# Edge softmax of the third graph layer: lanes of 128 edges, turned by TensorE, in place of a table in memory

## The reference

```
h = (x @ W.T).reshape(n, 8, 64)
e = leaky_relu(e_src + e_dst, 0.2)          # one number per edge and head
e = e * (1.0 + et_emb[edge_type]) * edge_weight[:, None]
e_max = zeros(n, 8).at[dst].max(e)          # maximum over the edges of a node, at least 0
e = exp(e - e_max[dst])
e_sum = zeros(n, 8).at[dst].add(e)
out = zeros.at[dst].add(h[src] * e / (e_sum[dst] + 1e-10)) + x
```

## Time and profile before

| | us |
|---|---|
| median of 3 runs | 1818.19 (1817.63 to 1823.83) |
| profiled execution | 1826.41 |
| its span, first to last instruction | 1824.3 |
| TensorE busy | 1594.4 (87%) |
| VectorE busy | 898.4 (49%) |
| GpSimd busy | 642.5 (35%) |

### The profile page before, as it was taken

The page is one execution under the profiler, slowest core; times in us unless marked ns, Lnnn a source line. Parts: engine busy times, 40 slices in busy tenths (PEclk is TensorE's granted clock), DMA queues, the critical chain, the costliest instruction groups (busy, mean ns, idle before and its releaser), DMA issues.

```text
span 1824.3 us, 23037 instructions
## 1 busy us (share of the span) xinstructions
PE 1594.4 (87%) x7110; PEld 880.6 (48%) x7111; DVE 898.4 (49%) x2199; ACT 501.0 (27%) x1607; POOL 642.5 (35%) x748
## 2 busy tenths in 40 slices
PE   6989999998697999999993496679699899999698
PEld 3534444446354546464551373524244455555455
DVE  8878888887634443433433035978722101011322
ACT  1134444446422414232230112411210211111233
POOL 5867787772332322223233812537500000000000
PEclk9999999998798999999996697579899999999899
DMA  7030101006323142222212572566515222210020
GB/s 308 4 103 24 58 24 58 24 7 169 84 71 125 53 90 78 79 84 56 86 37 87 131 250 79 163 149 186 162 69 190 69 75 69 98 58 23 10 60 18
DMA packets 132572, 162.75 MB, mean 89 GB/s; under 512 B 62041, under 2 KB 74601, under 8 KB 132114
## 3 DMA queue, kind: packets, MB, share of 16 engines
q1 hardware_dynamic: 105888, 116.45, 20.6%
q0 software_dynamic: 18752, 29.91, 6.2%
q10 hardware_dynamic: 7858, 15.44, 2.5%
HBM read 145.87 MB, written 15.88 MB: 89 GB/s over the span
## 4 chain that ended last, share of the span: by engine, by line
PE 69%; DMA 14%; DVE 11%; issue 3%; ACT 2%; POOL 1%; DVEq 0%; ACTq 0%; POOLq 0%
PE psum L377 68%; DMA tab_sorted<-rec,pos 12%; DVE arena L2586 2%; DVE stats L468 1%; DVE ring L1277 1%; PE psum L1008 1%; PE psum L2245 0%; POOL arena L624 0%; DMA arena<-tab_x 0%; DMA tab_x<-xn,gate 0%; POOL tab_x L2288 0%; ACT arena L2837 0%; DMA x<-in_x 0%; DVE xn L2038 0%; DVE mv L469 0%
## 5 line engine op out<-in xcount | busy, mean ns | idle before, releaser
L377 PE MATMUL psum<-arena 128*128 128x24 bf16 (+8 forms) x2026 | 325.8, 319 | 30.8 <-DVE arena L654 12.8
L377 PE MATMUL psum<-arena,ring 128*128 (+1 forms) x1504 | 325.4, 363 | 9.3 <-issue 6.2
L377 PE MATMUL psum<-xT,ring 128*128 128x384 f32 x928 | 319.4, 506 | 10.1 <-ACT ring L3020 4.2
L377 PEld LDWEIGHTS psum<-arena 128*128 128x128 bf16 (+5 forms) x2026 | 199.3, 149 | 163.5 <-issue 74.7
L377 PE MATMUL psum<-ring,arena 128*128 128x512 f32 (+1 forms) x592 | 271.1, 605 | 7.3 <-ACT arena L2837 3.8
L377 PE MATMUL psum<-ring,xT 128*128 128x512 f32 x552 | 252.3, 609 | 2.9 <-DMA bc<-in_wide 1.8
L377 PEld LDWEIGHTS psum<-xT,ring 128*128 128x128 f32 x928 | 182.4, 198 | 140.6 <-issue 30.0
L377 PEld LDWEIGHTS psum<-arena,ring 128*128 128x128 bf16 (+1 forms) x1504 | 139.2, 115 | 130.3 <-issue 28.9
L2128 POOL DMA_INDIRECT tab_sorted<-rec,pos x104 | 99.9, 961 | 242.6 <-DMA tab_sorted<-rec,pos 226.0
L1059 ACT ACTIVATE ring<-ring 128x128 f32<-128x128 f32 x416 | 123.3, 297 | 173.3 <-DVE ring L1343 173.3
L377 PEld LDWEIGHTS psum<-ring,arena 128*128 128x128 f32 (+1 forms) x592 | 102.6, 187 | 133.7 <-issue 132.6
(11 more groups left out here) (456 smaller groups left out, 1635.4 us busy)
## 6 DMA issues: line engine op xcount, KB each, us to landing
ring<-in_L_ffn_w SPq DMA_DIRECT2D x22, 1024.0 KB, 8.3
ring<-in_L_gnn_m_w SPq DMA_DIRECT2D x8, 1024.0 KB, 6.1
ring<-in_L_ffn_expert_weights SPq DMA_DIRECT2D x8, 1024.0 KB, 5.4
ring<-tab_key ACTq DMA_DIRECT2D x24, 256.0 KB, 3.2
ring<-in_L_gnn_Wv SPq DMA_DIRECT2D x5, 1024.0 KB, 5.1
tab_w<-xn SPq DMA_DIRECT2D x6, 768.0 KB, 14.4
ring<-in_L_gnn_Ww SPq DMA_DIRECT2D x4, 1024.0 KB, 17.1
ring<-in_L_gnn_wq SPq DMA_DIRECT2D x4, 1024.0 KB, 6.3
```

The source lines that it names most:

```text
L377: return nc.tensor.matmul(o, a, b, start=start, stop=stop)
```

## The change

- `rec` is no longer loaded for this layer; scores, factors and keys use `rec2`, so column T is tile T (25 groups still, the last of two tiles). `edge_factors` waits for the tile-wise load.
- The destination key is the number within its chunk. One compare instead of three serves it; TensorE picks the chunk's table with a register, loaded by `chunks_of` once a group, after the wait for the compares. A group has four compares and 16 matmuls of 24 columns.
- Leaky ReLU and factor: GpSimd does tiles 0 to 39 ahead of its gather 13, and tiles 40 to 79 ahead of gather 21 (four operations each); VectorE does the last 18 tiles, waiting for GpSimd (`factored`) ahead of its multiply.
- TensorE transposes the scores, eight times 128 x 98 to 98 x 128, into two banks; VectorE's scans read them there: 16 scans over 98 partitions x 128. The scan over lanes is 8 x 196.
- The joining is 16 operations of 98 x 128, in two halves of four heads; after each half come the subtraction, four transposes on TensorE and the exponential on ScalarE, which writes `w_tile`. `tab_weight`, its store and its two loads are gone.
- The clearing matmuls of the scatter and the first `hot` (7 tiles) with its bf16 form come earlier, beside the scans and the `l2m` step.

```diff
-        GG = EW // GT
+        GG = (TT2 + GT - 1) // GT
+        HH = H8 // 2
+        POOLED_SCORES = {13: (0, 10), 21: (10, 20)}
+        SCORED_LATE = GT * 20
@@ sp
-            sp.wait_ge(ex_done, 1)
-            sp.dma_start(tab_weight.rearrange("(p t) h -> p t h", p=P), weight[:]).then_inc(weights_stored, 16)
-            sp.wait_ge(weights_stored, 16)
...
-                sp.dma_start(w_tile[:, T0:T1, :], tiles_of_weights[:, T0:T1, :]).then_inc(weights_in[part], 16)
@@ pe, a group of scores
                 pe.wait_ge(nodes_ready, g + 1)
                 b = banks.open(pe, f"l2e{g}")
-                for j in range(GT):
-                    for f in range(2):
-                        for c in range(NT):
...
+                four = chunks_of(GT * g)
+                for j in range(min(GT, TT2 - GT * g)):
+                    o = b[:, j * 3 * H8:(j + 1) * 3 * H8]
+                    for c in range(NT):
+                        mm(o, node_hot[:, g % 2, c, j * P:(j + 1) * P], parts[:, 0, c, :, :].rearrange("p k h -> p (k h)"),
+                           c == 0, False)
+                    last = mm(o, node_hot[:, g % 2, NT, j * P:(j + 1) * P], dst_parts[:, bass.ds(four[j] * 3 * H8, 3 * H8)], False, True)
@@ pe, after the scores
             pe.wait_ge(lanes_ready, 1)
+            banks.at = SUMS + 1
+            for k in range(2):
+                b = banks.open(pe, f"l2t{k}")
+                for h in range(HH):
+                    last = nc.tensor.transpose(b[0:TT2, h * P:(h + 1) * P], w_edge[:, :, HH * k + h], ident[:])
+                last.then_inc(banks.full_of(f"l2t{k}"), 1)
+            pe_clear_sums(pe, "l2")
...
+            for k in range(2):
+                pe.wait_ge(lanes_ready, 4 + k)
+                b = banks.open(pe, f"l2v{k}")
+                for h in range(HH):
+                    last = nc.tensor.transpose(b[:, h * TT2:(h + 1) * TT2], weight[:, HH * k + h, :], ident[0:TT2, 0:TT2])
+                last.then_inc(banks.full_of(f"l2v{k}"), 1)
@@ act
-            act.wait_ge(lanes_ready, 3)
-            nc.scalar.activation(weight[:], weight[:], ACT.Exp).then_inc(ex_done, 1)
-            act_scatter_rows(act)
+            act_hot_half(act, 0)
+            for k in range(2):
+                b = banks.filled(act, f"l2v{k}")
+                nc.scalar.activation(w_tile[:, HH * k:HH * k + HH, :].rearrange("p h t -> p (h t)"), b[:, 0:HH * TT2],
+                                     ACT.Exp).then_inc(banks.free_of(f"l2v{k}"), 1)
+            for i in range(1, TT2 // RB):
+                act_hot_half(act, i)
@@ pool
+            def between(T):
+                if T not in POOLED_SCORES:
+                    return
+                g0, g1 = POOLED_SCORES[T]
+                banks.all_drained(pool, [f"l2e{g}" for g in range(g0, g1)])
+                own = slice(GT * g0, GT * g1)
+                small = sel8[:, own, :]
+                op.link(nc.gpsimd.tensor_scalar(small, w_edge[:, own, :], 0.0, 0.2, ALU.min, ALU.mult))
+                op.link(nc.gpsimd.tensor_scalar(w_edge[:, own, :], w_edge[:, own, :], 0.0, None, ALU.max))
+                op.link(nc.gpsimd.tensor_tensor(small, small, w_edge[:, own, :], ALU.add))
+                nc.gpsimd.tensor_tensor(w_edge[:, own, :], small, fac[:, own, :], ALU.mult).then_inc(factored, 1)
+            pool_scatter_rows(pool, tab_h, between)
@@ dve
+            late = slice(SCORED_LATE, TT2)
             dve.wait_ge(factor_ready, 1)
+            od.link(nc.vector.scalar_tensor_tensor(out=w_edge[:, late, :], in0=w_edge[:, late, :], scalar=0.2, in1=w_edge[:, late, :],
+                                                   op0=ALU.mult, op1=ALU.max))
+            dve.wait_ge(factored, len(POOLED_SCORES))
+            nc.vector.tensor_tensor(w_edge[:, late, :], w_edge[:, late, :], fac[:, late, :], ALU.mult).then_inc(lanes_ready, 1)
+            w_lane = [banks.filled(dve, f"l2t{k}")[0:TT2, :].rearrange("l (h p) -> l h p", h=HH) for k in range(2)]
             for h in range(H8):
+                own = w_lane[h // HH][:, h % HH, :]
+                nc.vector.tensor_tensor_scan(top[:, h, :], run[:, 0:P], own, MASKED, ALU.add, ALU.max)
+                last = nc.vector.tensor_tensor_scan(weight[:, h, ::-1], run[:, 1:P + 1][:, ::-1], own[:, ::-1], MASKED, ALU.add, ALU.max)
+            last.then_inc(lanes_ready, 1)
+            dve_hot_rows(dve, 0)
...
+            for k in range(2):
+                for s_ in range(2):
+                    for h in range(HH * k, HH * k + HH):
+                        last = nc.vector.scalar_tensor_tensor(out=top[:, h, :], in0=end_mask[:, s_, :],
+                                                              scalar=whole_max[:, s_ * H8 + h:s_ * H8 + h + 1], in1=top[:, h, :],
+                                                              op0=ALU.add, op1=ALU.max)
+                    od.link(last)
+                own = slice(HH * k, HH * k + HH)
+                nc.vector.tensor_tensor(weight[:, own, :], w_lane[k], top[:, own, :], ALU.subtract).then_inc(lanes_ready, 1)
             dve_scatter_rows(dve, od)
```

More of the change, by code:

```diff
@@ L216, in gnn_ffn_program @@
         rec2 = ranking[:].rearrange("p a b -> p (a b)")[:, 0:TT2 * 4].rearrange("p (t k) -> p t k", k=4)
+        dst2, typ2, ew2 = (rec2[:, :, k] for k in range(1, 4))
         tri_b = sb("tri_b", [P, P], BF16)
@@ L662, in dve_scatter_rows, with act_hot_half, chunks_of, pe_clear_sums @@
                                             ALU.subtract).then_inc(pieces_made, 1)
[L664 to L668, removed]
-                nc.scalar.activation(hot_half[:, i % 2], hot[:, i % 2], ACT.Copy).then_inc(bf16_made, 1)
-        def pe_scatter_rows(pe, tag):
+        def act_hot_half(act, i):
+            act.wait_ge(msg_used, RB * i + RB)
+            act.wait_ge(hot_rows, i + 1)
+            nc.scalar.activation(hot_half[:, i % 2], hot[:, i % 2], ACT.Copy).then_inc(bf16_made, 1)
+        def chunks_of(T):
+            _, some = nc.values_load_multi_w_load_instructions(
+                chunk2_i[0:1, T:min(T + 4, TT2)], engines=[mybir.EngineType.PE], min_val=0, max_val=NT - 1,
+                skip_runtime_bounds_check_because="a sum of two comparisons is 0, 1 or 2")
+            return some
+        def pe_clear_sums(pe, tag):
             banks.at = 0
@@ L703, in pe_scatter_rows @@
                     four = chunks_of(T + 1)
+            bk = [psum[:, c, :] for c in range(SUMS + 1)]
             for c in range(NT):
@@ L2564, in _ @@
+            V.tensor_scalar(run, run, MASKED, None, ALU.mult)
+            od.link(V.tensor_scalar(lane_flag[:, 0:2 * TT2 + 1], lane_flag[:, 0:2 * TT2 + 1], MASKED, None, ALU.mult))
         @on("dve")
@@ L2613, in _ @@
-            banks.drained(dve, "l2w")
-            for s_ in range(2):
-                od.link(nc.vector.tensor_tensor(sel8[:], end_mask[:, s_, :].unsqueeze(2).broadcast_to([P, EW, H8]),
-                                                whole_max[:, s_:s_ + 1, :].broadcast_to([P, EW, H8]), ALU.add))
-                od.link(nc.vector.tensor_tensor(top[:], top[:], sel8[:], ALU.max))
-            nc.vector.tensor_tensor(weight[:], w_edge[:], top[:], ALU.subtract).then_inc(lanes_ready, 1)
+            od.link(nc.vector.tensor_copy(whole_max, b[0:TT2, 0:2 * H8]))
@@ L2619, in _ @@
             dve_scatter_rows(dve, od)
             V = nc.vector
+            dve.wait_ge(lanes_ready, 5)
+            for k in range(2):
+                V.memset(gate[:, 15, 8 + k:9 + k], 0.0).then_inc(banks.free_of(f"l2t{k}"), 1)
             for t in range(NT):
```

178 lines of the change are left out of this document (83 added, 95 removed).

## The result

| | kernel before | changed kernel |
|---|---|---|
| median of the runs beside each other | 1821.01 us (1816.8 to 1825.9, 6 runs) | 1810.4 us (1802.17 to 1810.84, 6 runs) |
| ratio, 95% interval | | 0.993 [0.9902, 0.9957] |
| the profiled execution | 1826.41 us, span 1824.3 | 1802.17 us, span 1800.4 |

The changed kernel is faster by 0.4 to 1.0%: 0.7%, which is 12.7 us of the 1818.2 of the prediction and puts the changed kernel at 1805.5 there, where 1802.6 was forecast. The two medians alone lie 10.6 us apart. The two profiled executions lie 24.2 us apart, about twice the ratio's figure, so the pair must be cut at landmarks before it is read. Four are used from here on: **C**, VectorE's first compare; **R**, the start of the last operation ahead of the scans (before: of the first scan); **S**, the scatter's first matmul; **G**, the start of GpSimd's last gather. The stage is C to G.

What follows compares the result with a forecast made beforehand. VectorE's scores, then the weights' store and load, then a gather-bound scatter were taken as the bounding chain. An earlier scatter start (12.9) plus a shorter scatter (2.7) gave 15.6 us off 1818.2: 1802.6, 8-in-10 range 1796 to 1813.

Steps and rivals of the forecast that it cites:

- The scores: Score loop: VectorE's four compares and a reduction set the pace, 1.4 us a group, VectorE done at 1167.6.
- The register loads: TensorE in the score loop: about 0.5 us a group, covered by 0.41 to 0.86 us of queued spreading matmuls.
- rival B: Score loop: register load not covered, 1.95 us a group on TensorE at the low clock, 5.7 us off, 1812.5; chance 0.14.
- GpSimd's blocks: Leaky ReLU and factors on GpSimd: 4.2 us a block, 8.4 for two, ending at 1171.3, after VectorE's scores.
- SyncE's queue: Biases and expert weights load earlier, onto the first gathers: 1.5 us (0 to 3) on GpSimd's way to its second block.
- From the scores to the scatter: Transposes, scans, lane step, joining and exponential: from scores ready at 1171.6 to the scatter at 1190.2, before 1203.08.
- the two halves: Joining before the scatter: eight operations at 0.2 us in a row and a subtraction per half, 4.8 us together.
- The scatter: First matmul to last gather: bound by gathers at 1.407 us, 96.2 against 98.96 us, 2.7 gained (0 to 4).
- Rival A: GpSimd's blocks and VectorE's compares hold each other up, VectorE ending last: 10.9 us gained, 1807.3; chance 0.17.
- Rival C: Score loop: a long uncovered register load, 1.3 us, makes a group 2.75 us and the kernel slower, 1832.5; chance 0.07.
- Rival D: More gained: GpSimd blocks of 3.0 us, no crowding, VectorE's scores decide: 19 to 20 us off, 1799; chance 0.10.
- Nothing elsewhere: Outside the stage no cost: 0.6 us more prologue and `edge_factors` maybe 10 us later are covered by waits.

Runs made afterwards that it cites:

- e8: Changed kernel with VectorE doing all leaky ReLU and factors, chunk registers loaded before the wait, scans starting after four transposes: 1800.98 us, ratio 0.9911.
- e9: Changed kernel with the chunk registers loaded before TensorE's wait for the compares, GpSimd keeping its blocks: 1811.36 us, ratio 0.9931.
- e6: Changed kernel with the destination key compared with all three chunks again (six compares, 24 products, no register load): 1820.21 us, ratio 1.0012.
- e7: Changed kernel with GpSimd's two blocks removed, VectorE doing all leaky ReLU and factors: 1806.83 us, ratio 0.9934.
- the controls: The changed kernel without a further edit, in two undisturbed profiles: last score 36.4 and 37.3 us after the first compare.
- e10: Changed kernel with SyncE issuing the next layer's biases and expert weights only after the softmax's last subtraction: 1806.15 us, ratio 0.9897.
- sets 2 to 4: The three later groups of runs, without the slow score loop: kernel before, changed kernel and edited versions; ratios to the kernel before 0.9897 to 1.0019.
- e5: Changed kernel with VectorE doing all leaky ReLU and factors and GpSimd's first gather waiting for the last score compares: 1821.15 us, ratio 1.0009.
- c1: The changed kernel run again with no edit but asserted register values: 1807.78 us, ratio 0.9936.
- set 1: First group of runs, with a disturbed score loop: changed kernel (1846.68 us) and three one-edit versions; ratios to the kernel before 0.9829 to 0.9924.
- e2: Changed kernel with the chunk registers loaded before TensorE's wait for the compares, in the disturbed runs: 1843.03 us, ratio 0.9829.
- b0: The kernel before, run and profiled again with no edit but asserted register values: 1821.25 us, ratio 1.0019.

## Why the prediction was right, point by point

*The scores*, forecast at 1.4 us a group and VectorE done 36.6 us after C. Measured 1.352, and 36.4 and 37.3 us. The pace is VectorE's in the main, as the sum had it: its window is full, with about 1.18 us for four compares and 0.17 for a reduction. Not wholly: e8 and e9, with the register load moved, ran at 1.23 to 1.26 us a group, so about 0.1 us was TensorE's, although VectorE's row shows no idle time for it. The total also contains two things that the step did not have: 2.1 us lost beside the first block (below), and the load ahead of the first products, which puts the first score 0.7 us later than forecast. That it agrees to within 1 us is in part luck: a pace below the 1.4 taken made up for both. e6 shows what this step is worth: with six compares the last score is back at 50.3. Of the 14 us by which the stage shrank, the one-chunk compare with its products carries 10 (157.3 against e6's 167.5); the rest of the change carries 3 to 3.5 us of the stage (170.4 and 171.0 against 167.5), most of it in the scatter, which the times do not resolve.

*The register loads*, forecast at 0.5 us and covered. Shown wrong in size: the gap ahead of the first products is 0.93 us, twice, in two kernels, and the first products of e8 start 0.8 us sooner after C. Inside the loop it is covered only in part: e8 against e7 gives 2.8 us, e9 against the controls 2.1 to 3.0, about 0.1 us a group. It never reached the 1.95 us a group of rival B, and that was not for want of a low clock. Two groups of the changed kernel (scores at 1151.31 and 1154.00, columns as above) ran wholly at B's 0.50:

```profile
1151.31:1154.00 2.69, 2.69 (x51) 2.68 (x50) 2.61 (x11) 2.25 (x5) 2.08 (x3) 0.50 0.69 200
```

That is 1.35 us a group with TensorE busy throughout. B's sum had 1.40 for the matmuls alone and added the load to them; here the load added nothing. Nor did the load touch the sum, since GpSimd ended later (e9). The Trainium skill gives 600 ns as the floor of a `tensor_load` ("DMA: Bandwidth & Descriptors", "Latency and other measured facts"); the rows agree that it is a floor, with 0.93 for four behind a wait.

*GpSimd's blocks*, 4.2 us each and last to end, 40.3 us after C (1171.3). Measured 4.5 (1143.28 to 1147.79) and 4.3, R at 41.4 and 41.1, VectorE idle before it. The step named the right joint; e7 priced it at 3.2 to 4.6 us.

*SyncE's queue*, crowding of 1.5 us on GpSimd's way: 2.05 at gather 4, and e10 gives back 2.3 to 2.7 at R.

*From the scores to the scatter*, forecast 18.6 us from the end of the late multiply; measured 19.7. Transposes 1.95, as forecast. Scans 5.1 for 5.2. The mis-sized term is the two halves:

```profile
1174.28 2.04 DVE L2658 SCALAR_TENSOR_TENSOR arena<-arena 98x128 f32<-98x128 f32 x7
1176.36 0.69 DVE L2663 TENSOR_TENSOR arena<-psum,arena 98x512 f32<-98x512 f32 x1
1176.97 2.30 DVE L2658 SCALAR_TENSOR_TENSOR arena<-arena 98x128 f32<-98x128 f32 x8
1179.31 0.69 DVE L2663 TENSOR_TENSOR arena<-psum,arena 98x512 f32<-98x512 f32 x1
```

They take 6.0 us (1174.02 to 1180.00), not 4.8: an operation goes every 0.29 us, not every 0.2. The earlier trace rows had 280 ns for the same size, and the step discounted it for standing in a row; there was nothing to discount.

*The scatter*, 96.2 us: measured 94.4 and 96.2. The size was right. The step gave two reasons, the expert weights and the tail of the weight table. Of the first alone e10 shows that it costs nothing when issued 2.2 us ahead of S: 94.3 and no wait at gather 36. The second is gone in every kernel with the shorter scatter (94.3 to 96.2 in sets 2 to 4, but for e5). Which of the two made the wait of 2.74, or whether it took both at once, was not tried.

*Rival A* is partly real. Against 1.13 us, four compares took 0.57 and 0.97 longer beside the first block and the next 0.57 again, 2.1 us for 4.5 of block. How much depended on GpSimd's operation. Beside the first, with one input (1143.28, 1.39 us), three compares got through, at 0.53 to 0.55 us each instead of the usual 0.34 (in c1 and e6 one of 0.82 and 0.83 and then shorter ones). Each of the two with two inputs held up a single compare for about its whole length:

```profile
1145.98 1.02 DVE L2622 TENSOR_SCALAR arena<-arena,node_id 128x512 bf16<-128x512 f16 x1
1146.00 0.86 POOL L2552 TENSOR_TENSOR arena<-arena 128x320 f32<-128x320 f32 x1
1147.09 0.85 DVE L2622 TENSOR_SCALAR arena<-arena,node_id 128x512 bf16<-128x512 f16 x1
```

c1, e6 and e10 show the same, with single compares of 0.85 to 1.03 us. The full blocking that the Trainium skill states in "SBUF — State Buffer", "Summary: rules for kernel authors", therefore agrees with the trace for the two-input operations and not for the one-input ones, during which several compares ended. So half of A's sign came (single compares over 0.6 us), and the other half, VectorE never idle before the late multiply, did not: only the first block lay beside the scores. In e6, where both did, they cost VectorE about 4.5 us of 9.2. *Rival C* did not occur undisturbed, and set 1 is not its mechanism: the long gaps there were between single matmuls, not ahead of the products, and e2 without the load behind the wait had them too. *Rival D* is what the kernel does once the joints are opened: e8 starts the scatter 54.0 us after C, 7 earlier. What D named, shorter blocks and no crowding, is not how: the blocks were taken away.

*Nothing elsewhere* held: GpSimd's `edge_factors` began about 5 us later against the gathers that follow it, where 10 were allowed for, and GpSimd was still idle for 38 us ahead of these (before 42.8):

```profile
1090.90 1.08 POOL L621 DMA_INDIRECT arena<-tab_eo,gate  x1 [38.01 <-DMA tab_eo<-arena]
```

The forecast was 3 us too low against 1805.5. The scatter started 1.9 to 2.2 us later than forecast (59.2 after C): 0.8 to 1.1 at R, and 1.1 behind it, where the halves alone took 1.2 more. The scatter's own 0 to 1.8 us below its 96.2 took some of that back; the rest is within what the runs can tell.

## What to carry to other kernels

When two edits come in one change, price them apart: here the cheaper compares carried about 10 of 14 us, and all the rest bought a scatter start 0.7 to 0.8 us earlier (e6). The trip through memory was 5.4 us long in the chain, but the transposes and the longer chain in its place took most of that: from R to S it is 20.0 us in e6 and was 21.3 and 21.8. GpSimd's blocks saved 1.8 us between the last score and R there (0.9 instead of 2.7) and lost more than that ahead of it. A helper engine takes work off a bound one only if its own queue lets it finish earlier: GpSimd's two blocks spared VectorE two operations of 0.98 us, slowed its compares by 2.1 us, and were waited for 3.75. And opening one joint of a chain shows nothing while the next is closed (load ahead: 2 to 3 us at the score, none at the scatter), so look at the idle time of the engine behind it before giving an edit up.

## What the runs showed of the hardware, unexpectedly

- The same program had a score loop of 36.4 and of 59.1 us. In the long one TensorE had nothing to wait for in the records and yet started one to four matmuls every 0.7 to 1.7 us in the rows shown, while indirect gathers kept the DMA engines 0.63 to 0.73 busy (0.81 in the short one); with the DMA share at 0.01 the matmuls came close together again. It was there in all four kernels of one set and in none of the others, on the same chip among them. The cause is open.
- The clock granted to one loop is not a property of the kernel: the score loop of the kernel before had 0.50 in one profile (TensorE 11.18 of 13.00 us busy) and 0.97 in the next (8.90 of 13.00), and the loop's length differed by 0.5 us. What made the difference the runs do not show.
- VectorE's compares (fp16 in, bf16 out) took 0.34 us alone and 0.33 to 0.83 beside a one-input GpSimd operation of 1.4 us, during which several ended; beside a two-input one of 0.86 us there was each time a single compare, of 0.85 to 1.03.
- Indirect gathers went every 1.25 us at the closest. Into free buffers the mean was 1.28 to 1.35 (before, b0, e5, e7, waits included), into buffers in use 1.37 to 1.42, whether the expert weights were loaded early or around the scatter's start (e10), and also when all gathers started late (e5).
